# Window loads of 192 rows in halves of TensorE, two bias rows behind the filter, and another order of one pipeline step

## The reference

```python
h = relu(layernorm(x))
# layer 0, senders = src, receivers = dst
basis = gaussian_smearing(edge_weight)                 # 50 functions of the distance
ef = shifted_softplus(basis @ Wf1 + bf1) @ Wf2 + bf2
messages = (h @ W_lin.T)[src] * ef
agg = segment_sum(messages, dst)
x = x + shifted_softplus(agg @ Wm1 + bm1) @ Wm2 + bm2
# layer 1, row = src, col = dst
h = relu(layernorm(x))
out = h @ W_self.T + b_self
neigh = h[dst] @ W_neigh.T + b_neigh
x = x + out + segment_sum(neigh, src) / max(count(src), 1)
```

## Time and profile before

| | before |
|---|---|
| median of three runs | 1936.53 us |
| the profiled execution's own time | 1934.63 us |
| its span | 1932.4 us |
| TensorE busy | 1740.7 us (90%) |
| VectorE busy | 1463.5 us (76%) |
| GpSimd busy | 1138.4 us (59%) |
| ScalarE busy | 1122.0 us (58%) |
| DMA moved | 372.54 MB, 193 GB/s in the mean |

### The profile page before, as it was taken

How to read it: one execution, slowest core, us unless ns; L and a number is a source line. 1 busy time by engine, 2 the same in 40 slices (tenths; PEclk the granted TensorE clock), 3 DMA queues, 4 the chain that set the end, 5 groups by cost and what they waited for, 6 DMA issues and landing times. The chain is left out here.

```text
span 1932.4 us, 46473 instructions
## 1 busy us (share of the span) xinstructions
PE 1740.7 (90%) x11686; PEld 1343.8 (70%) x11686; DVE 1463.5 (76%) x4618; ACT 1122.0 (58%) x2713; POOL 1138.4 (59%) x938
## 2 busy tenths in 40 slices
PE   2659679999999999999999999999999845888998
PEld 1223257777777777777777777777777645888897
DVE  8989547877777777777777877777877625777886
ACT  1017668877777777777777777777764312333333
POOL 6970244366666666666666666666653363556676
PEclk9769769999999999999999999999999987999999
DMA  2000045677777777777777767677767556999876
GB/s 79 0 1 1 28 112 160 204 223 240 231 225 234 228 223 237 235 223 235 228 223 235 235 205 214 212 204 212 220 195 213 156 163 193 274 279 285 250 221 177
DMA packets 342167, 372.54 MB, mean 193 GB/s; under 512 B 40508, under 2 KB 269758, under 8 KB 342078
## 3 DMA queue, kind: packets, MB, share of 16 engines
q1 hardware_dynamic: 265246, 293.99, 51.2%
q0 software_dynamic: 25088, 51.83, 8.9%
q10 hardware_dynamic: 51744, 25.70, 4.4%
HBM read 251.54 MB, written 119.82 MB: 192 GB/s over the span
## 5 line engine op out<-in xcount | busy, mean ns | idle before, releaser
L764 POOL DMA_INDIRECT xg<-in_x,srcs x392 | 435.3, 1110 | 440.8 <-issue 362.0
L775 POOL DMA_INDIRECT row_table<-row_out,posq x392 | 387.3, 988 | 194.7 <-issue 125.8
L1231 PE MATMUL psum<-bin_rows,bin_hot 128*128 128x129 f32 x2352 | 288.6, 281 | 47.9 <-DVE bin_hot L1204 47.8
L1231 PEld LDWEIGHTS psum<-bin_rows,bin_hot 128*128 128x128 f32 x2352 | 274.0, 194 | 62.6 <-issue 30.8
L1102 PEld LDWEIGHTS psum<-hwin,hotT 128*128 128x128 f32 x1568 | 186.9, 195 | 78.3 <-issue 68.8
L1004 ACT ACTIVATE nhT<-psum 128x512 f32<-128x512 f32 x98 | 58.5, 597 | 309.8 <-PE psum L1074 309.8
L887 DVE TENSOR_TENSOR hotT<-dst_keys,reach 128x1024 f32<-128x1024 int32 x98 | 120.8, 1232 | 139.5 <-PE psum L1102 138.2
L1102 PE MATMUL psum<-hwin,hotT 128*128 128x128 f32 x1568 | 204.4, 285 | 15.6 <-DMA hwin<-h_table 9.9
L1091 PE MATMUL psum<-hot,win 128*128 128x128 f32 x1568 | 191.6, 275 | 1.4 <-DVE hot L859 1.4
L1091 PEld LDWEIGHTS psum<-hot,win 128*128 128x128 f32 x1568 | 183.4, 192 | 1.6 <-DVE hot L859 1.6
L1204 DVE TENSOR_TENSOR bin_hot<-iota,bin_rel 128x1536 f32<-128x1536 f32 x98 | 174.4, 1779 | 5.3
(11 more groups left out here) (174 smaller groups left out, 3761.9 us busy)
## 6 DMA issues: line engine op xcount, KB each, us to landing
win<-msg_table SPq DMA_DIRECT2D x392, 129.0 KB
hwin<-h_table SPq DMA_DIRECT2D x392, 128.0 KB
bin_rows<-row_table SPq DMA_DIRECT2D x196, 195.0 KB, 3.2
msg_table<-msgw SPq DMA_DIRECT2D x98, 258.0 KB, 4.0
nx<-in_x_nodes SPq DMA_DIRECT2D x98, 256.0 KB, 4.1
h_table<-h1s SPq DMA_DIRECT2D x98, 256.0 KB
dst_keys<-in_dst_rows SPq DMA_DIRECT2D x98, 256.0 KB
y_table<-ys SPq DMA_DIRECT2D x61, 256.0 KB, 4.1
```

What stands on the lines that cost most here:

```text
L764: nc.gpsimd.indirect_dma_start(out=xg[:, par, t, :], out_offset=None, in_=ins["x"], in_offset=bass.IndirectOffsetOnAxis(ap=srcs[:, par, t: ...
L775: nc.gpsimd.indirect_dma_start(out=row_dram, out_offset=bass.IndirectOffsetOnAxis(ap=posq[:, par, t:t + 1], axis=0), in_=row_out[:, par, t ...
L1231: last = nc.tensor.matmul(bank[2 * slot + b][:, h * MW:(h + 1) * MW], bin_hot[:, slot % 2, b, w, h * P:(h + 1) * P], bin_rows[:, slot, b, ...
```

## The change

The windows have `SPAN` = 192 rows instead of 256. A window is loaded into 64 partitions, three rows in each: even tiles of a quad into the lower half of the partitions, odd ones into the upper. `block_sums` and `edge_rows` then make three products of 64 rows per tile instead of two of 128, even and odd tiles in turn, and these write to two different PSUM banks (bank 4 for even tiles, bank 5 for odd ones, `agg` in the first 256 columns of each and `rows` in the last 256). The one-hot tiles shrink from 1024 to 768 columns and are double-buffered. `mlp_ps`, `self_ps` and `neigh_ps` are now one bank. The bias row is split from `product`; those of `mlp` and of `filt` are issued directly behind the filter, and take their three rows from the half that the filter doesn't use in that step. TensorE's and ScalarE's lists have another order.

```diff
-SPAN = 2 * P
+HALF = P // 2
+WT = 3
+SPAN = WT * HALF
...
-                u_ps, turn_ps, proj_ps, filt_ps, agg_ps, nu_ps, mlp_ps, self_ps = bank
-                neigh_ps, rows_ps = self_ps, agg_ps
+                u_ps, turn_ps, proj_ps, filt_ps, _, _, nu_ps, node_ps = bank
+                self_ps = mlp_ps = neigh_ps = node_ps
+                agg_at, rows_at = 0, 2 * P
+                def half_of(t):
+                    return slice(HALF * (t % 2), HALF * (t % 2) + HALF)
+                def tile_ps(at, t):
+                    return bank[4 + t % 2][:, at + t // 2 * P:at + t // 2 * P + P]
...
-                            sp.dma_start(win[:, par, k, :, :].rearrange("p w c -> p (w c)"),
-                                         msg_dram[bass.ds(start, SPAN), :].rearrange("(p w) c -> p (w c)", p=P)).then_inc(win_loaded[par], 16)
+                            sp.dma_start(win[half_of(k), par, k // 2, :, :].rearrange("p w c -> p (w c)"),
+                                         msg_dram[bass.ds(start, SPAN), :].rearrange("(p w) c -> p (w c)", p=HALF)).then_inc(win_loaded[par], 16)
...
-                        sp.dma_start(dst_keys[:, par, :], ins["dst_rows"][q, :].partition_broadcast(P)).then_inc(x_keys[par], 16)
+                        for h in range(2):
+                            sp.dma_start(dst_keys[half_of(h), par, :], ins["dst_halves"][q, h, :].partition_broadcast(HALF)).then_inc(x_keys[par], 16)
...
                         if there(s - 9):
                             clamp(s - 9, nu_ps[:], bm1_top, nclamp[:], n_u, n_clamp)
+                        if there(s - 18):
+                            rows_out(s - 18, even)
+                        if there(s - 12):
+                            hidden_out(s - 12, even)
                         if there(s - 11):
                             evacuate(s - 11, nhT[:], turn_ps[:], n_turned, n_neigh, n_hT, ACT.Relu)
-                        if there(s - 12):
-                            hidden_out(s - 12, even)
-                        if there(s - 18):
-                            rows_out(s - 18, even)
...
+                    def bias_row(q, ps, b, at, used):
+                        wait_used(pe, used, q, 1)
+                        nc.tensor.matmul(ps[:], ones3[at:at + 3, :], bias3[at:at + 3, b, :], start=True, stop=False)
...
-                        for k in range(QT):
-                            for w in range(2):
-                                last = nc.tensor.matmul(agg_ps[:, k * P:(k + 1) * P], win[:, par, k, w, 0:C], hot[:, k, w, :],
-                                                        start=(w == 0), stop=(w == 1))
+                        for g in range(2):
+                            for w in range(WT):
+                                for h in range(2):
+                                    last = nc.tensor.matmul(tile_ps(agg_at, 2 * g + h), win[half_of(h), par, g, w, 0:C], hot[half_of(h), par, g, w, :],
+                                                            start=(w == 0), stop=(w == WT - 1))
...
                         if there(s):
                             filter_up(s, even, pair, slot)
+                        beside = HALF - BASIS_AT[even]
+                        if there(s - 9):
+                            if there(s - 11):
+                                pe.wait_ge(n_y, s - 11 + 1)
+                            bias_row(s - 9, mlp_ps, 1, beside, n_x1)
+                        if there(s - 1):
+                            bias_row(s - 1, filt_ps, 0, beside, e_filter_sb)
```

More of the change, by code:

```diff
@@ L405, in _ @@
                 link(nc.vector.tensor_reduce(out=violations[:, 4:5], in_=bad[:], axis=AX.X, op=ALU.add))
[L406 to L407 removed]
+                for h in range(2):
+                    half = slice(HALF * h, HALF * h + HALF)
+                    for w in range(WT):
+                        nc.vector.tensor_scalar(reach[half, :, w], firsts[half, :].rearrange("p (g h) -> p h g", h=2)[:, h, :],
+                                                iota3[half, w:w + 1], None, ALU.add)
                 link(nc.vector.tensor_tensor(bad[:], curf[:], nxtf[:], ALU.is_gt))
@@ L1099, in edge_rows @@
                         wait_used(pe, x_rows, q, 1)
-                        for t in range(QT):
-                            for w in range(2):
-                                last = nc.tensor.matmul(rows_ps[:, t * P:(t + 1) * P], hotT[:, t, w, :], hwin[:, par, t, w, :],
-                                                        start=(w == 0), stop=(w == 1))
+                        for g in range(2):
+                            for w in range(WT):
+                                for h in range(2):
+                                    last = nc.tensor.matmul(tile_ps(rows_at, 2 * g + h), hotT[half_of(h), par, g, w, :], hwin[half_of(h), par, g, w, :],
+                                                            start=(w == 0), stop=(w == WT - 1))
                         last.then_inc(x_sum, 1)
@@ L1117, in step @@
                             nc.tensor.matmul(nu_ps[:], wm1[:], aggs[:], start=True, stop=True).then_inc(n_u, 1)
-                        if there(s - 11):
-                            pe.wait_ge(n_y, s - 11 + 1)
-                            product(s - 11, neigh_ps, nhT, wneigh, 3, n_hT, n_hn, n_neigh)
-                        if there(s):
-                            filter_up(s, even, pair, slot)
-                        if there(s - 17):
-                            if there(s - 8):
-                                pe.wait_ge(n_aggT, s - 8 + 1)
-                            edge_rows(s - 17, odd)
                         if there(s - 10):
@@ L1133, in step @@
                             turn(nxn, n_turned)
-                        if there(s - 2):
-                            product(s - 2, proj_ps, hT, wlin, None, e_hT, e_msg, e_proj)
+                        if there(s - 11):
+                            pe.wait_ge(n_y, s - 11 + 1)
+                            if there(s - 9):
+                                pe.wait_ge(n_x1, s - 9 + 1)
+                            bias_row(s - 11, neigh_ps, 3, 0, n_hn)
+                            product(s - 11, neigh_ps, nhT, wneigh, True, n_hT, n_hn, n_neigh)
                         if there(s - 1):
-                            product(s - 1, filt_ps, su, wf2, 0, e_soft, e_filter_sb, e_filter)
+                            product(s - 1, filt_ps, su, wf2, True, e_soft, e_filter_sb, e_filter)
                             pe.wait_ge(e_norm, s - 1 + 1)
```

92 lines of the change are left out of this document (55 added, 37 removed).

## The result

The changed kernel takes 2145.9 us (median of four runs, 2137.17 to 2147.5) against 1937.19 us before: 1.107 times as long (95% interval 1.103 to 1.110). I had predicted 2026 us with a range from 1855 to 2110. The direction and the place of the new wait were right, the size was not: more than half of the increase was missing.

A forecast was written before the change was run, and what follows sets the result against it. It took TensorE's own work to bound the kernel before, at 13.16 us a step, and a 14.23 us loop through ScalarE afterwards; +90 us on the profiled 1934.63 gave 2024, predicted as 2026 us, 8-in-10 range 1855 to 2110.

The forecast's parts named there:

- Prices of TensorE's work: TensorE's matmul groups priced from the profile before, at 0.1125 us per pass and 0.10 per switch: 12.12 us a step.
- Rivals 1 and 2: Bias rows run beside the filter: 1970 us, chance 0.20; halves don't run beside each other: 2240 us, chance 0.13.
- The loop through h1s, aggs, hT, wlin and neigh: Through ScalarE and TensorE once per step: 6.33 us up to wlin plus 7.90 to neigh's end, 14.23 against 13.16 before.
- ScalarE's long wait: On ScalarE, 3.02 us ahead of nhT before; expected to move to h1s and be ended by neigh.
- Rivals 3 and 4: Loop doesn't bind, TensorE's 12.12 us is the period: 1841 us, chance 0.20; errors make loop equal old period: 1936, 0.04.
- From h1s to aggs ... less 0.48 for row_out, which now stands ahead: ScalarE's stretch from h1s to aggs: 4.34 us, or 5.57 in steps that also make the basis.
- the term for the block sums: aggs must also wait for TensorE's block sums, 4.81 us after neigh's end, counting from nhT done at 1.10.
- The sum: Whole kernel: 81 full steps +87 us, 6 early steps +9, last 8 steps -7, first stage +0.5, together +90.
- The steps ahead of `edge_rows`: The 6 steps before edge_rows begins: 11.3 us each before, 12.8 after, +9 us.
- The end: The last 8 steps, without filter and wlin, have no wlin to wait for: about 0.9 us less each, -7 us.

The follow-up runs named there:

- halves_apart: Changed kernel in the old order, biases ahead of their products, with all block_sums and edge_rows products of even tiles before those of odd ones: 2050.3 us, ratio 1.056.
- bias64: Changed kernel with the two bias rows behind the filter given 64 rows instead of 3, the others zero: 2055.8 us, ratio 1.062.
- order_alone: Kernel before with only the new order of TensorE's and ScalarE's lists, windows still 256 rows: 2152.2 us, ratio 1.113.
- fill4: Changed kernel with four extra products (8 passes, results overwritten by wlin) ahead of TensorE's wait for hT: 2076.1 us, ratio 1.071.
- wlin_back: Changed kernel with the product with wlin moved back behind the turn of comb: 2171.2 us, ratio 1.122.
- late: Halves with edge_rows, turn of comb and wlin behind nu, filter directly behind block_sums, biases moved, ScalarE's list as before: 2291.4 us, ratio 1.183.

## Why the prediction was wrong, step by step

- *Prices of TensorE's work*: right. `block_sums` 1.54 with both switches (forecast 1.55), `edge_rows` 1.45 (1.45), filter with its switch 0.95 (0.96), two biases 0.53 (0.52). halves_apart shows that it takes alternating halves, and bias64 that the two biases cost their 0.53 only because of their row count. Rivals 1 and 2 are out. The rule of the Trainium skill, "TensorEngine Tiling (Array Packing)", Key Properties, that changing the mode drains the engine and changing only the tile doesn't, agrees: two biases of 3 rows behind 50 cost 0.53 more than two of 64 rows beside 50.
- *The loop through h1s, aggs, hT, wlin and neigh*: right. order_alone makes it by itself, and TensorE is busy 85% as forecast. One sign was read wrongly: ScalarE's long wait did not move to h1s. It stands ahead of nclamp (5.65 us, for nu), and h1s waits 0.75 for neigh; it is the short wait that closes the loop. Rivals 3 and 4 are out.
- *"From h1s to aggs ... less 0.48 for row_out, which now stands ahead"*: wrong. Where row_out left the stretch, nhT came in, with nearly the same 0.47 (907.73 to 908.20 after). I had the two lists in front of me and took out one name without putting in the other, although the term for the block sums has nhT right behind h1s (done at 1.10). A small error came on top: h1s starts 0.11 behind neigh's last pass (922.67 + 1.16 to 923.94), where I had 0.03. In steps without the basis the missing 0.48 hardly shows, since the forecast had aggs wait for the block sums until 4.84, which is what ScalarE's corrected stretch comes to: fill4's period there is 13.97 (forecast 13.85). With the basis it is 15.18 (14.61). That is (0.12 + 0.57)/2 = 0.35 a step.
- *The missing term: the clock*. The sum took every duration at clock 1.00 although it added waits of 1.1 us and, in basis steps, of 1.9 us (6.71 - 4.81) to an engine that had none. After the changed kernel's long waits it fell to 0.50 each time. fill4 shows that this, and not the wait, costs 0.79 a step.
- *The sum*: 81 steps with 87 us forecast, 81 x 0.35 = 28 for ScalarE and 81 x 0.78 = 63 for the clock (15.35 - 14.57, both from edge_rows to filter) make 178; 177.5 were measured. The steps ahead of `edge_rows` lost 20.6 instead of 9 (0.9 of the 21.5 are the first stage's): wlin waits for hT in 16 of them, 25.6 us in all, and the mean clock from 221 to 410 us is 0.79, against 0.84 before from 220 to 389. The end lost 4 instead of gaining 7: its steps take 10.28 us against 10.33, because `edge_rows` now waits 0.70 us for aggs in each, and the last loads of hwin are waited for 14.9 us in all against 9.9. How the clock and the waits divide the 20.6 was not measured.
- *Range and rivals*: no rival was "the wait costs more than its length". With the longer of two alternating waits worked out (1.9 us) instead of the mean (1.5), I should have asked what an idle TensorE does next.

What stays open: what decides whether the clock falls behind a given wait of 2.1 to 2.5 us, when, and for how long. In one kernel it falls behind each of them, in two others behind about every second, of the same length to 0.1 us, and a fall costs from 1.6 to 4.9 us. One thing speaks against pure chance: in the middle of the changed kernel one fall begins 30.72 us behind the last, in order_alone 61.44, twice that, although their loops differ by 0.37 us a step. No run here changed one such thing alone.

## What to carry to other kernels

A saving on the busiest engine is worth nothing if the new order closes a loop through another engine: write the loop out, from an instruction back to itself one step later, with both lists of the changed code beside each other, and count what came into the stretch as well as what left it. Where a wait appears on TensorE, price the matmuls behind it at either clock level; extra passes ahead of the wait, which do nothing, can be cheaper than idling. And a part of a change that loses as a whole may be a gain: the halves were worth 2.4% in the old order and, with the biases, one turn and row_out moved, 5.3%.

## What the runs showed of the hardware

- Between 520 and 1300 us TensorE's granted clock never fell behind an idle stretch under 1.4 us in any of these kernels. Behind those of 2.1 to 2.5 us it fell 25 times of 25 (changed kernel), 13 of 26 (order_alone), 13 of 27 (bias64) and 22 of 23 (wlin_back, where it stayed up behind the one of 1.9 us), and behind those of 2.9 to 3.2 us 46 times of 46 (late). A fall began between 0.2 us before the wait's end and 1.7 us after it.
- Twelve f32 products of 64 rows (24 passes) in alternating halves take 1.54 us with the switches, in halves one after the other 2.53.
- A 50-row product in one half, 64-row products in the other and a 64-row bias run beside each other; a 3-row bias does not, and costs 0.53 us for two where 64 rows cost nothing.
